# Layers 2 to 4 of a graph convolution: source terms as two float32r parts in a 128-column stationary

## The reference, cut to what matters

```python
for l in range(4):
    hw = h @ Ws[l]
    agg = jnp.zeros_like(hw).at[dst].add(enorm * hw[src])   # enorm = dinv[src] * dinv[dst]
    agg = agg + self_norm * hw + bs[l]
    mean = jnp.mean(agg)
    var = jnp.mean(jnp.square(agg - mean))
    h = relu(ln_w[l] * (agg - mean) * jax.lax.rsqrt(var + EPS) + ln_b[l])
```

## Time and profile before

| | |
|---|---|
| median of 3 runs | 11015.86 us |
| span of the profiled execution | 11011.8 us |
| its own time, span and what lies around it | not given apart from the three runs; the median is 4.1 us over the span |
| busy: PE, DVE, ACT, POOL | 7985.6, 6439.8, 5694.1, 5298.0 us |
| mean granted TensorE clock | 0.780 |
| q1 (all loads of `adj`, and others) | 1293.70 MB of 1737.34 MB |

### The profile page before, as it was taken

How to read it: one execution, slowest core, us unless ns; L and a number is a source line. 1 busy time by engine, 2 the same in 40 slices (tenths; PEclk the granted TensorE clock), 3 DMA queues, 4 the chain that set the end, 5 groups by cost and what they waited for, 6 DMA issues and landing times.

```text
span 11011.8 us, 201943 instructions
## 1 busy us (share of the span) xinstructions
PE 7985.6 (73%) x67921; PEld 5571.5 (51%) x67921; DVE 6439.8 (58%) x17837; ACT 5694.1 (52%) x8457; POOL 5298.0 (48%) x5426
## 2 busy tenths in 40 slices
PE   3444444428888888346656896599999999986999
PEld 2333333326667666234545664356656656554555
DVE  6777777737666666265777775444343344343444
ACT  1111111115555555235233885488888878864777
POOL 5777777757777777757777777610000000000000
PEclk6555555557776777577678998799999999997999
DMA  4555555533333333989589675566666666645998
GB/s 150 171 166 170 167 172 167 170 58 93 92 93 92 93 93 93 55 198 273 139 183 215 185 204 136 129 190 206 205 186 205 205 184 206 205 146 105 175 169 163
DMA packets 2775008, 1737.34 MB, mean 158 GB/s; under 512 B 1811302, under 2 KB 2613708, under 8 KB 2774036
## 3 DMA queue, kind: packets, MB, share of 16 engines
q1 hardware_dynamic: 2434836, 1293.70, 47.7%
q10 hardware_dynamic: 165920, 277.72, 7.0%
q0 software_dynamic: 173408, 154.46, 6.3%
HBM read 1065.63 MB, written 502.11 MB: 142 GB/s over the span
## 4 chain that ended last, share of the span: by engine, by line
POOL 37%; PE 33%; issue 18%; DMA 6%; DVE 3%; ACT 2%; SPq 1%; POOLq 0%; DVEq 0%; ACTq 0%
PE PS L1146 29%; POOL adj L780 14%; POOL records L736 11%; POOL G L706 10%; DMA AG<-adj 2%; DMA G<-node_table,IDX 1%; DMA IDX<-in_src_q 1%; DMA records<-RT,IDX 1%; PE PS L1020 1%; DVE OH L1776 1%; POOL AG L754 1%; ACT AG L1637 1%; PE PS L860 0%; DVE S L1783 0%; PE PS L1174 0%
## 5 line engine op out<-in xcount | busy, mean ns | idle before, releaser
L1146 PE MATMUL PS<-AG,T 128*64 128x512 bf16 (+1 forms) x22096 | 2577.0, 355 | 280.3 <-DVE Hn L2236 97.3
L1543 ACT CAST AG<-AG 128x1792 bf16<-128x1792 uint8 x1176 | 1971.1, 1683 | 322.1 <-DMA AG<-adj 232.7
L780 POOL DMA_INDIRECT adj<-OH,EA x1664 | 1639.7, 985 | 589.6 <-issue 589.6
L706 POOL DMA_INDIRECT G<-node_table,IDX x1664 | 1627.9, 978 | 599.9 <-issue 587.7
L736 POOL DMA_INDIRECT records<-RT,IDX x1664 | 1614.6, 970 | 543.6 <-issue 497.1
L1146 PEld LDWEIGHTS PS<-AG,T 128*64 128x64 bf16 x22096 | 1269.1, 110 | 1125.4 <-issue 142.9
L2143 DVE CAST AG<-AG 128x1792 bf16<-128x1792 uint8 x882 | 964.9, 1094 | 1492.0 <-PE PS L1146 1227.7
L1146 PE MATMUL PS<-AG,RT 128*64 128x512 bf16 (+1 forms) x11048 | 1519.5, 354 | 0.0
L1543 ACT CAST M<-AG 128x1792 bf16<-128x1792 uint8 x588 | 990.6, 1685 | 352.8 <-PE PS L1146 271.6
L1020 PE MATMUL PS<-R 98*128 98x128 f32 x3328 | 995.7, 392 | 0.0
L1783 DVE TENSOR_TENSOR_SCAN S<-M,S,PS 128x512 f32<-128x512 bf16 x621 | 791.9, 1275 | 235.0 <-ACT PS L1472 205.5
(11 more groups left out here) (376 smaller groups left out, 13843.5 us busy)
## 6 DMA issues: line engine op xcount, KB each, us to landing
AG<-adj SPq DMA_DIRECT2D x2940, 224.0 KB
adj<-Z ACTq DMA_DIRECT2D x105, 1568.0 KB
G<-records SPq DMA_DIRECT2D x624, 128.0 KB
M<-same_dst SPq DMA_DIRECT2D x416, 128.0 KB
fill_rows<-Z ACTq DMA_DIRECT2D x104, 512.0 KB, 2.9
runs_l<-R SPq DMA_DIRECT2D x208, 256.0 KB
G<-fill_rows SPq DMA_DIRECT2D x208, 256.0 KB
M<-same_src SPq DMA_DIRECT2D x416, 128.0 KB
```

The lines of the kernel that those rows point to most:

```text
L706: pool.indirect_dma_start(G[:, i, q * D:(q + 1) * D], None, table, bass.IndirectOffsetOnAxis(ap=IDX[:, i, q:q + 1], axis=0)).then_inc(sem( ...
L780: pool.indirect_dma_start(adj_cells, bass.IndirectOffsetOnAxis(ap=CELL[:, at:at + 1], axis=0), VAL[:, at:at + 1], None).then_inc(sem(f"cel ...
L1146: m = pe.matmul(PS[h * D:(h + 1) * D, base + c:base + c + w], stat(t), rhs[:, h * QW + c:h * QW + c + w], start=start and t == 0, stop=sto ...
L1543: act.copy(RING[i], RAW[i]).then_inc(sem("conv_a"), 1)
```

## The change

In layers 2 to 4 the source terms are kept as two parts of type float32r, side by side in one stationary of 128 columns (64 of the upper part, 64 of the lower), the bytes are converted to float32r, and a tile takes 4 matmuls over the full width of the array: 2 halves of the destinations x 2 column pieces. The upper part's sum falls into PSUM partitions 0 to 63, the lower part's into 64 to 127, for each half of the destinations apart (4 banks for a group, and the other 4 for the next). They are joined per group: ACT copies one 64-partition part of each half to the other partitions (`shift`), DVE adds (`join`), then scales and takes the statistics as before. `own_r` takes 14 matmuls of 128 columns.

The conversions are dealt out anew: ACT two of five, DVE three. There are seven byte buffers (`NW`) and five float32r ring buffers, which lie in space of `EA`, `G`, `R`, `RT` and `OH`; so the 98 gathers into `EA` wait for the end of layer 4 (`group_done`), and POOL's gathers of virtual rows go to `VR`. At the start of a layer SP issues seven loads ahead of the seven table writes. The splitting has one step less on ACT and one less on DVE.

```diff
@@ SP @@
-            def adj_in(u, g, r, i):
...
+            def adj_in(it, g, v, q):
+                sp.wait_ge(*conv_at((q - NW) % NR, it * NW + (q - NW) // NR))
+                sp.dma_start(RAWF[q % NW][:, :], adj[bass.ds(v * (STEP * P) + q * P, P), bass.ds(g * (2 * QW), 2 * QW)])\
+                  .then_inc(sem(f"ring_in{q % NW}"), 16)
...
             with sp.Fori(1, LAYERS) as l:
+                it = l * LI - LI
+                for q in range(NW):
+                    adj_in(it, 0, 0, q)
                 layer_table(l)
-                for i in range(NR):
-                    adj_in(l * NG2, 0, 0, i)
...
+                for q in range(NW, STEP):
+                    adj_in(it, 0, 0, q)
+                for g in range(NG2):
+                    with sp.Fori(0 if g else 1, GI) as v:
+                        for q in range(STEP):
+                            adj_in(it + (g * GI + v), g, v, q)
+                    group_end(l * NG2 + g, g, g % 2)
@@ POOL @@
+            with pool.Fori(1, LAYERS) as l:
+                virtual_rows(l, VR)
+
             for x in range(2):
                 pool.wait_ge(sem(f"e_out{x}"), 8 * NCH)
+            pool.wait_ge(sem("group_done"), LAYERS * NG2)
             for g in range(NG):
...
@@ PE @@
+            def dense(l, g, x):
...
+                for K in range(AB):
+                    v, q = K // STEP, K % STEP
+                    pe.wait_ge(*conv_at(q % NR, (it + (g * GI + v)) * NW + q // NR))
...
+                    stat = TERMSR[:, K * 2 * D:(K + 1) * 2 * D] if K < NJ else VTR[:, (K - NJ) * 2 * D:(K - NJ + 1) * 2 * D]
+                    for h in range(2):
+                        for c, w in SPLIT:
+                            o = (4 * x + 2 * h) * 512 + c
+                            m = pe.matmul(PS[:, o:o + w], stat, RINGF[q % NR][:, h * QW + c:h * QW + c + w],
+                                          start=K == 0, stop=False, skip_group_check=True)
+                    m.then_inc(sem("ring_free"), 1)
...
+            def own_r(g, x):
+                for h in range(2):
+                    for b in range(GT):
+                        j = (g * 2 + h) * GT + b
+                        o = (4 * x + 2 * h) * 512 + b * P
+                        m = pe.matmul(PS[:, o:o + P], TERMSR[:, j * 2 * D:(j + 1) * 2 * D], ident_r[:, :],
+                                      start=False, stop=True, skip_group_check=True)
+                m.then_inc(sem("group_done"), 1)
@@ ACT @@
+            def to_f32r(it, q0, q1):
+                for q in range(q0, q1):
+                    if q % NR in F_ACT:
+                        act.wait_ge(*raw_at(it, q))
+                        act.wait_ge(sem("ring_free"), it * STEP + (ONCE + q + 1))
+                        act.copy(RINGF[q % NR][:, :], RAWF[q % NW][:, :]).then_inc(sem("conv_a"), 1)
...
+            def shift(l, g):
+                act.wait_ge(sem("group_done"), l * NG2 + g + 1)
+                act.wait_ge(sem("joined"), l * (2 * NG2) + (2 * g + 4 - 2 * NG2))
+                for h in range(2):
+                    o = (4 * (g % 2) + 2 * h) * 512
+                    act.copy(SHIFT[h * D:(h + 1) * D, :], PS[(1 - h) * D:(2 - h) * D, o:o + QW]).then_inc(sem("shifts"), 1)
@@ DVE @@
+                        dve.tensor_copy(RINGF[q % NR][:, :], RAWF[q % NW][:, :]).then_inc(sem("conv_d"), 1)
...
+            def join(l, g, h):
+                o = (4 * (g % 2) + 2 * h) * 512
+                dve.wait_ge(sem("shifts"), l * (2 * NG2) + (2 * g + h + 1 - 2 * NG2))
+                if h == 0:
+                    dve.wait_ge(sem("group_done"), l * NG2 + g + 1)
+                dve.tensor_tensor(cols(FM, g)[h * D:(h + 1) * D, :], PS[h * D:(h + 1) * D, o:o + QW],
+                                  SHIFT[h * D:(h + 1) * D, :], ALU.add).then_inc(sem("joined"), 1)
...
                 for g in range(1, NG2):
-                    to_bf16(l * NG2 + g, 0)
-                    scaled(l, g - 1)
-                    with dve.Fori(1, NK) as r:
-                        to_bf16(l * NG2 + g, r)
-                statistics(l, scaled(l, NG2 - 1))
+                    to_f32r(it + g * GI, 0, NR)
+                    join(l, g - 1, 0)
+                    to_f32r(it + g * GI, NR, NR + 2)
+                    join(l, g - 1, 1)
+                    to_f32r(it + g * GI, NR + 2, NR + 4)
+                    scale_r(l, g - 1)
+                    to_f32r(it + g * GI, NR + 4, NR + 6)
+                    stats_r(l, g - 1)
+                    to_f32r(it + g * GI, NR + 6, STEP)
+                    with dve.Fori(1, GI) as v:
+                        to_f32r(it + (g * GI + v), 0, STEP)
```

More of the change, by code:

```diff
@@ L27 @@
 F32 = mybir.dt.float32
+F32R = mybir.dt.float32r
 BF16 = mybir.dt.bfloat16
@@ L116, in sem, with here, over @@
             return sems[name]
+        def here():
+            return -(-nc.sbuf_base // 32) * 32
+        def over(name, shape, dt, at):
+            return nc.alloc_sbuf_tensor_at(name, shape, dt, offset=at)
         X = sb("X", [P, NJ * D])
         Hn = sb("Hn", [P, NJ * D])
+        T_AT = here()
         T = sb("T", [P, NJ * D])
@@ L791, in _, with virtual_rows @@
             ends(AG, runs64, endrow[1], NG)
[L792 removed]
+            def virtual_rows(l, rows):
                 for s in range(3):
@@ L797, in virtual_rows @@
                 for k in range(NV):
-                    pool.indirect_dma_start(VT[:, k * D:(k + 1) * D], None, table,
+                    pool.indirect_dma_start(rows[:, k * D:(k + 1) * D], None, table,
                                             bass.IndirectOffsetOnAxis(ap=srow[:, k:k + 1], axis=0)).then_inc(sem("vt_in"), 16)
@@ L817, in _ @@
                                             bass.IndirectOffsetOnAxis(ap=endrow[1][:, j:j + 1], axis=0)).then_inc(sem(f"ends_e{s}"), 16)
-            with pool.Fori(1, LAYERS) as l:
-                virtual_rows(l)
             pool.wait_ge(sem("table_out"), TP + 16)
@@ L1220, in _ @@
                 for g in range(NG2):
-                    dense(l * NG2 + g, g % 2, g == 0, l)
-                    own(g, g % 2)
+                    dense(l, g, g % 2)
+                    own_r(g, g % 2)
                 total(0, l * 2 + 1)
@@ new lines, in virtual_r, with split_r @@
+            def virtual_r(l):
+                act.wait_ge(sem("vt_in"), l * (16 * NV) + 16 * NV)
+                act.activation(VTR[:, :].rearrange("p (k t d) -> p k t d", t=2, d=D)[:, :, 0, :],
+                               VR.rearrange("p (k d) -> p k d", d=D), ACT.Copy, scale=float(FULL)).then_inc(sem("vt_hi"), 1)
+            def split_r(l):
+                act.wait_ge(sem("pcols_ready"), l + 1)
+                act.sem_inc(sem("turns"), 1)
+                for g in range(NG2 + 1):
+                    if g < NG2:
+                        hidden(g, None, (sem("proj"), l * NG2 + g - 1) if g >= 2 else None)
+                    if g >= 1:
+                        act.wait_ge(sem("tt_ready"), l * NG2 + g)
+                        act.copy(part_r(g - 1)[:, :, 0, :], TT[(g - 1) % 3].rearrange("p (j d) -> p j d", d=D)).then_inc(sem("hi"), 1)
@@ new lines, in shift @@
+            def shift(l, g):
[4 more added lines that the diff above has]
+                    act.copy(SHIFT[h * D:(h + 1) * D, :], PS[(1 - h) * D:(2 - h) * D, o:o + QW]).then_inc(sem("shifts"), 1)
+            with act.Fori(1, LAYERS) as l:
+                split_r(l)
+                it = l * LI - LI
+                with act.Fori(0, GI - 1) as v:
+                    to_f32r(it + v, 0, STEP)
+                virtual_r(l)
+                to_f32r(it + (GI - 1), 0, STEP)
+                for g in range(1, NG2):
+                    to_f32r(it + g * GI, 0, NR)
+                    shift(l, g - 1)
+                    to_f32r(it + g * GI, NR, STEP)
+                    with act.Fori(1, GI) as v:
+                        to_f32r(it + (g * GI + v), 0, STEP)
+                shift(l, NG2 - 1)
@@ new lines, in stats_r @@
+            def stats_r(l, g):
+                dve.wait_ge(sem("group_used"), l * NG2 + g + 3)
+                for k, (c, w) in enumerate(SPLIT):
+                    f = cols(FM, g)[:, c:c + w]
+                    if g == NG2 - 1 and k == 1:
+                        dve.bn_stats(BN[0:D, 2 * g + k, :], f[0:D, :])
+                        t = dve.bn_stats(BN[D:P, 2 * g + k, :], f[D:P, 0:w - (NP - n_nodes)])
+                    else:
+                        t = dve.bn_stats(BN[:, 2 * g + k, :], f)
+                return t
@@ new lines, in _ @@
+            with dve.Fori(1, LAYERS) as l:
+                split_r(l)
+                it = l * LI - LI
+                with dve.Fori(0, GI - 1) as v:
+                    to_f32r(it + v, 0, STEP)
+                virtual_r(l)
+                to_f32r(it + (GI - 1), 0, STEP)
+                for g in range(1, NG2):
+                    to_f32r(it + g * GI, 0, NR)
+                    join(l, g - 1, 0)
[7 more added lines that the diff above has]
+                    with dve.Fori(1, GI) as v:
```

(5 more changed lines are left out.)

159 lines of the change are left out of this document (99 added, 60 removed).

## The result

The changed kernel took 10365.1 us (median of 4 runs, 10362.42 to 10379.58), the kernel before 11014.4 us: a ratio of 0.9414 (95% interval 0.9401 to 0.9428), 649 us less. The forecast was 10260 us with a range of 10165 to 10510. The profiled execution was the longest of the four (10379.58 us, span 10377.8).

The account below looks back on a forecast made before the run. PE was taken to bound the dense part. A layer of 885.8 - 260 + 3 + 9 + 3 - 7 = 634 us is 252 less, 756 over three layers: 11015.9 - 756 = 10260 us, range 10165 to 10510.

Parts of the forecast that it names:

- The PE term: Dense tiles: four full-width float32r matmuls run at bfloat16's rate per column, 0.756 us a tile on PE.
- The boundaries: Between groups: joins and scaling on DVE delay conversions, +1.5 us for each of 6, 9 us a layer (0 to 18).
- Behind the last group: A layer's end: one copy and two joins ahead of the scaling, with nothing to cover them, +3 us.
- Splitting: Splitting the source terms: DVE's three passes a group become two and ACT loses one, -7 us a layer.
- Own terms: The `own_r` matmuls: 14 of 128 columns in place of 21 pairs, +3 us over 7 groups (-3 to +13).
- The gathers: The 98 gathers, moved behind layer 4: covered by the 225 us before DVE needs them, cost 0.
- SP's waits: Group boundaries: SP waits for `group_used` with loads queued behind, but it is given early, cost 0.
- Rival 1: Dense tiles: loads become the bound at 0.87 us a tile, 10460 us; casts wait mostly for DMA; chance 0.20.
- Rival 2: Dense matmuls: float32r is read at one float32 instruction's pace, 1.50 us a tile, 11830 us; chance 0.09.
- Rivals 3 and 4: DVE's cast loses its double pace, 11190 us, chance 0.03; float32r runs like float32, above 15000, chance 0.01.

Follow-up runs that it names:

- e6: Changed kernel with bfloat16 in place of float32r, and loads of 64 bytes a row from tile 36 of a layer on: 0.756 us a tile, 13935.54 us.
- e3: Changed kernel with conversions of only 64 of 1792 columns from each layer's second group on: 0.817 us a tile, 10340.57 us.
- e4: Changed kernel with loads of only 64 of 1792 bytes a row from tile 36 of each layer on: 0.817 us a tile, 10346.44 us.
- e8: Changed kernel with a layer's first seven loads put back behind the table writes: 27.2 us instead of 24.4 to the first dense matmul, 14092.79 us.
- e1: Changed kernel with bfloat16 in place of float32r for terms, converted tiles and identity: 10365.0 us.
- e11: Changed kernel with a later group's shifts, joins, scaling and statistics dealt out over more conversions: 10343.22 us, ratio 0.9386 to the kernel before.

## Why the prediction was right, and where it was off

The side, the mechanism and the order of size were right, and the time fell inside the range: 649 us less of 756 forecast. For a layer 252 us were forecast and 214.5 came, 37 less. Of its signs, three were missed: a layer of 620 to 650 us (671.3), 0.216 us for 512 columns (0.233) and, by little, 280 to 300 GB/s (275). The sum for the upper end of the range has a slip: 10460 with the boundaries at 18 instead of 9 is 10487, and 10510 is reached only with the upper bound of the own terms too.

- **The PE term was mis-sized, and with it the pace of a tile.** "Four full-width matmuls of the same lengths, at the same rate per column, take 4 x 0.189 = 0.756 us" holds for bfloat16 (e6: 0.756). float32r takes 0.817 (e3, e4, with loads or conversions out of the way). Against the 0.78 that I took for the tile this is 735 x 0.037 = 27 us a layer, the largest part. My lower bound stood in for the value because nothing in the trace of before lay between it and 1.50.
- **The boundaries.** 9 us were taken for six, with 0 to 18 as bounds; they cost 6 x 2.9 = 17, 8 more. The step said that the work is covered on average but falls on some fifteen tiles: that is where it fell. What it missed was that the first tiles' loads come late there, behind two other loads (e3, e4).
- **Behind the last group** +3 were taken and 14.5 - 9.4 = 5.1 came. Of the difference 1.4 is a longer pause of ACT ahead of `hidden`, which the trace puts down to issue (2.7 us idle, against 1.4 before); what causes it was not tried.
- **Splitting**: -7 forecast, -6.0 measured, 2.8 of it by the early loads (e8).
- **Own terms**: +3 forecast; 1.51 us instead of 21 x 0.056 = 1.18 make 7 x 0.33 = +2.3, 1 less.
- **The gathers** at 0, and SP's waits at 0: held as to the waits. But the term had only SP's wait for `group_used` in it, and not the two loads of `dinv_n` that stand behind the wait; by the traces they cost through the boundaries, which no run tried by itself. The later stretch of 225 us was kept, with POOL's gathers in it (busy for 126.5 us), and DVE did not wait for them:

```profile
9198.00:9423.00 225.00, 95.24 (x494) 84.80 (x494) 101.00 (x126) 39.66 (x43) 126.51 (x104) 0.56 0.23 45
```

27 for the pace, 8 for the boundaries, 2 behind the last group and 1 for the splitting, less 1 for the own terms, are the 37 us. The first group's slow stretches add nothing to that: before the change it lost 5 us against the others too, within the 885.8.

*Rival 1* (loads at 0.87) was wrong in its size, yet near: half of its sign came, conversions that wait mostly for loads, while PE hardly waited. Loads supply a tile in 0.80 us in a good stretch and 0.815 on average (e1), 0.3 to 2% below what float32r wants. The forecast had 0.77 for a full share at 297 GB/s; e1 reached 286. Two limits so near each other cost little in a steady stretch (0.820 us a tile on average and not 0.817), but they leave no room at a group's start, and with that the average tile of a later group took (90.2 - 1.5) / 105 = 0.845 us. *Rival 2* (the read of a 4-byte operand at half pace) is excluded: 0.233 us for 512 columns, not 0.43. The figure of the Trainium skill for the moving operand ("SBUF — State Buffer", A bandwidth-pool intuition that's wrong), 2 bytes a lane at 2.4 GHz, which it gives for bf16, is exceeded here: 4 bytes x 512 / 0.233 us are 8.8 GB/s a lane, against the 4.8 that it makes. *Rivals 3 and 4* are excluded by DVE's 1092 ns a conversion and by the pace.

Still open: why a float32r column costs 8% more than a bfloat16 one, and what the boundaries would cost with the loads of `dinv_n` elsewhere in the queue or with more than seven byte buffers. Stationaries of 64 float32r columns side by side in the two column halves, as the kernel before has them in bfloat16, weren't tried on the chip.

## What to carry to other kernels

When a change takes the limit off one engine, put the next limits beside it with their own measured pace: here PE at 0.817, the loads at 0.80 to 0.815 and the conversions at 2 x 1.59 / 5 = 0.64 and 3 x 1.00 / 5 = 0.60 us decided what halving the matmuls' columns could bring, and taking PE's last 7% (e1) brought nothing. Work that an in-order engine does once a group is free only if it is dealt out in steps smaller than the buffers between the engines; moving four steps apart by seven tiles gave 33 us (e11). Loads that are no tiles belong in the count of the queue too: two of them a group, by the traces, took the lead of the conversions just ahead of that work. And read an engine's pace from starts of back-to-back instructions, since durations overstated ACT's by 6% and DVE's by 9%.
